# Gate scan: the final norm of both halves of the images done in turn at the end, instead of the first half's inside the last units of the scan

## What is computed

```
y = jnp.einsum('bdchw,d->bchw', out_y, w_m)
y = layernorm2d(y, ln_w, ln_b)      # (x - mean_c) / sqrt(var_c + 1e-5) * w + b, per pixel over 96 channels
y = grn(y, grn_gamma, grn_beta)     # Gx = sqrt(sum_hw x^2); Nx = Gx / (mean_c Gx + 1e-6)
                                    # gamma * x * Nx + beta + x
return conv1x1(y, W_out)            # 96 -> 48 channels
```

## Time and profile before

| | |
|---|---|
| time, median of 3 runs | 1013.42 us (1012.63 to 1014.58) |
| time of the profiled execution | 1012.31 us |
| span of the profiled execution | 1010.4 us |
| TensorE busy | 826.8 us (82%) |
| VectorE busy | 796.4 us (79%) |
| ScalarE busy | 573.6 us (57%) |
| GpSimd busy | 244.6 us (24%) |
| granted TensorE clock, mean | 0.866 of full speed |
| first products of unit 5, 6, 7 | 882.35, 912.97, 945.75 us |
| first final addition (L1021) | 969.47 us |

### The profile page before, as it was taken

The page is one execution under the profiler, slowest core; times in us unless marked ns, Lnnn a source line. Parts: engine busy times, 40 slices in busy tenths (PEclk is TensorE's granted clock), DMA queues, the critical chain, the costliest instruction groups (busy, mean ns, idle before and its releaser), DMA issues.

```text
span 1010.4 us, 20810 instructions
## 1 busy us (share of the span) xinstructions
PE 826.8 (82%) x8186; PEld 565.8 (56%) x8188; DVE 796.4 (79%) x2001; ACT 573.6 (57%) x859; POOL 244.6 (24%) x272
## 2 busy tenths in 40 slices
PE   3799999999999999999999988889577667353544
PEld 2577877887788778877777775365121111031222
DVE  8788888888888888888888874655539999888852
ACT  1376677676776776676666663123565664746002
POOL 6122222222222222222222221292201222115201
PEclk8799999999999999999999997979777755565656
DMA  8100000000000000002000000100003675566300
GB/s 234 49 2 2 2 2 2 2 1 2 2 2 2 2 2 2 2 1 102 1 3 2 2 2 1 47 1 1 1 1 63 126 133 114 100 123 125 77 2 16
DMA packets 11622, 34.14 MB, mean 34 GB/s; under 512 B 1879, under 2 KB 4359, under 8 KB 11271
## 3 DMA queue, kind: packets, MB, share of 16 engines
q0 software_dynamic: 5904, 21.24, 11.2%
q1 hardware_dynamic: 5623, 11.60, 3.9%
HBM read 10.81 MB, written 0.79 MB: 11 GB/s over the span
## 4 chain that ended last, share of the span: by engine, by line
PE 63%; DVE 22%; ACT 5%; issue 5%; POOL 2%; DMA 2%; POOLq 0%; SPq 0%; DVEq 0%; ACTq 0%
PE narrow L1453 5%; PE scores_a L1425 4%; PE wide L1376 4%; PE scores_b L1425 4%; PE last L1530 4%; PE scores_b L1412 3%; PE scores_a L1436 3%; PE scores_b L1436 3%; PE scores_a L1412 3%; PE narrow L1472 3%; PE narrow L1483 3%; DVE prod L991 3%; DVE prod L999 2%; PE last L1526 2%; PE wide L1516 2%
## 5 line engine op out<-in xcount | busy, mean ns | idle before, releaser
L376 POOL TENSOR_TENSOR stb<-stb,neg_half 128x4 f32<-128x4 f32 x48 | 48.3, 1006 | 266.1 <-DVE stb L679 266.1
L1104 ACT ACTIVATE d<-d 128x768 f32<-128x768 f32 x96 | 80.6, 839 | 18.1 <-DVE d L626 17.6
L1453 PEld LDWEIGHTS narrow<-v,pt 128*64 128x64 f32 x2304 | 78.7, 137 | 13.4 <-issue 13.4
L1453 PE MATMUL narrow<-v,pt 128*64 128x54 f32 x2304 | 84.9, 224 | 0.1
L371 POOL TENSOR_TENSOR sta<-sta,neg_half 128x4 f32<-128x4 f32 x48 | 48.8, 1017 | 115.7 <-DVE sta L566 115.7
L1111 ACT ACTIVATE pt<-scores_a 128x768 f32<-128x768 f32 x48 | 38.8, 809 | 56.7 <-PE scores_a L1436 56.7
L607 DVE COPY v<-narrow 64x96 f32<-64x96 f32 x192 | 49.0, 255 | 18.8 <-PE narrow L1388 13.8
L1120 ACT ACT_TABLE_LOAD x47 | 60.3, 1283 | 0.8
L1104 ACT ACT_TABLE_LOAD x46 | 59.0, 1283 | 0.8
L613 DVE TENSOR_REDUCE mx<-scores_a 128x12 f32<-128x768 f32 x48 | 46.0, 957 | 16.4 <-PE scores_a L1425 16.4
L1080 ACT ACTIVATE xa<-narrow,wts 113x256 f32<-113x256 f32 x48 | 27.0, 564 | 52.6 <-PE narrow L1363 27.8
(11 more groups left out here) (330 smaller groups left out, 2268.6 us busy)
## 6 DMA issues: line engine op xcount, KB each, us to landing
gsum<-mag POOLq DMA_DIRECT2D x14, 512.0 KB, 4.7
ysum<-yo POOLq DMA_DIRECT2D x7, 768.0 KB, 5.8
ysum<-xd POOLq DMA_DIRECT2D x6, 768.0 KB, 6.0
gsum<-mag POOLq DMA_DIRECT2D x14, 256.0 KB, 4.6
wts<-in_wpack SPq DMA_DIRECT2D x6, 442.0 KB, 6.9
sed_w<-in_sed_in SPq DMA_DIRECT2D x1, 2304.0 KB, 8.0
graw<-in_gates_in SPq DMA_DIRECT2D x1, 1152.0 KB, 5.0
x_all<-in_x_tok SPq DMA_DIRECT2D x8, 96.0 KB, 3.2
```

Source lines behind the costliest of these rows:

```text
L1104: act.activation(d, d, ACT.Exp).then_inc(p_ready[u], 1)
L1453: op = pe.matmul(y_ps[64 * b:64 * b + 64, q * VO:(q + 1) * VO], t.pt[:, q, h, 64 * b:64 * b + 64], t.v[:, q, b, h * VO:(h + 1) * VO], star ...
```

## The change

Half 0 is no longer normed inside units 5 to 7. All six TensorE stages, five VectorE stages and three ScalarE stages of both halves come after unit 7, stage by stage, half 0 then half 1. To let them be under way together, `tvar`, `rT` and `gx` exist twice, half 1's `yq` is a part of a gate tile (`gate[0][:, 0, :]`), half 1 uses banks 0 and 1 (scores_a) where half 0 uses 6 and 7, and each half has its own semaphores. TensorE's wait of half 1 for half 0's copies becomes one for ScalarE's having taken the last gate maps from banks 0 and 1. GpSimd issues the powers as both of `tail_rstd`, then both of `tail_norms`.

```diff
-        tvar = sb("tvar", [128, 2, 16])
-        rT = sb("rT", [16, 128])
-        gx = sb("gx", [128, 6, 8])
+        tvars = [sb(f"tvar{i}", [128, 2, 16]) for i in range(2)]
+        rTs = [sb(f"rT{i}", [16, 128]) for i in range(2)]
+        gxs = [sb(f"gx{i}", [128, 6, 8]) for i in range(2)]
+        yqs = [yq, gate[0][:, 0, :]]
+TAIL_BANK = (6, 0)
...
@@ GpSimd
-                if u == 5:
-                    tail_rstd(0)
-                if u == 6:
-                    tail_norms(0)
...
-            tail_rstd(1)
-            tail_norms(1)
+            for hb in range(2):
+                tail_rstd(hb)
+            for hb in range(2):
+                tail_norms(hb)
@@ VectorE, unit(u)
-                if u == 6:
-                    tail(0, (2,))
...
-                if u in (5, 6):
-                    tail(0, (0,) if u == 5 else (3,))
...
-                if u in (5, 6):
-                    tail(0, (1,) if u == 5 else (4,))
...
-            tail(1, range(5))
+            for stage in range(5):
+                tail(0, (stage,))
+                tail(1, (stage,))
@@ ScalarE
-                if u in (6, 7):
-                    tail(0, (u - 6,))
                 first_guess(u)
-            tail(0, (2,))
-            tail(1, (0, 1, 2))
+            for stage in range(3):
+                tail(0, (stage,))
+                tail(1, (stage,))
@@ TensorE
                     else:
-                        pe.wait_ge(out_ready, 2)
+                        for k in range(2):
+                            pe.wait_ge(gate_taken[k], (24, 21, 21)[k])
...
                 in_gates(u)
-                if u >= 5:
-                    tail(0, ((0,), (3,), (5,))[u - 5])
                 if u < 7 and u != 3:
                     gates(u + 1, (1, 2))
-                if u in (5, 6):
-                    tail(0, (1,) if u == 5 else (4,))
...
-                if u == 5:
-                    tail(0, (2,))
-            tail(1, range(6))
+            for stage in range(6):
+                tail(0, (stage,))
+                tail(1, (stage,))
```

More of the change, by code:

```diff
@@ L253, in build @@
         sum_ready = sems("sum_ready", 2)
-        tail_pe, tail_dve = sem("tail_pe"), sem("tail_dve")
-        yq_ready, trstd_ready, v_norm, gx2_ready, gx_ready, out_ready = (
-            sem(n) for n in ("yq_ready", "trstd_ready", "v_norm", "gx2_ready", "gx_ready", "out_ready"))
+        tail_pe, tail_dve = sems("tail_pe", 2), sems("tail_dve", 2)
+        tail_act, tail_pool = sems("tail_act", 2), sems("tail_pool", 2)
         block = ctx.enter_context(nc.Block())
@@ L1049, in tail @@
-                    step(dve.tensor_scalar(gx[:, 2, 0:2], B8[7][:, 0:2], 1.0 / DIN, 1e-6, ALU.mult, ALU.add))
-                    step(dve.reciprocal(gx[:, 3, 0:2], gx[:, 2, 0:2]))
-                    step(dve.tensor_tensor(per_group(4), per_group(1), gx[:, 3, 0:2].unsqueeze(1).to_broadcast([128, G, 2]), ALU.mult))
+                        return gxs[hb][:, k, 0:6].rearrange("p (g b) -> p g b", b=2)
+                    dve.wait_ge(tail_pe[hb], M_GM + 1)
+                    step(dve.tensor_scalar(gxs[hb][:, 2, 0:2], B8[TAIL_BANK[hb] + 1][:, 0:2], 1.0 / DIN, 1e-6, ALU.mult, ALU.add))
@@ L1052, in tail @@
+                    step(dve.reciprocal(gxs[hb][:, 3, 0:2], gxs[hb][:, 2, 0:2]))
+                    step(dve.tensor_tensor(per_group(4), per_group(1), gxs[hb][:, 3, 0:2].unsqueeze(1).to_broadcast([128, G, 2]), ALU.mult))
                     step(dve.tensor_tensor(per_group(2), per_group(4), l3w[:, Q_GRN:Q_GRN + G].unsqueeze(2).to_broadcast([128, G, 2]), ALU.mult))
-                    step(dve.tensor_scalar(gx[:, 5, 0:6], gx[:, 2, 0:6], 1.0, None, ALU.add))
+                    step(dve.tensor_scalar(gxs[hb][:, 5, 0:6], gxs[hb][:, 2, 0:6], 1.0, None, ALU.add))
@@ L1806, in tail @@
                             first = 512 * g + 128 * t
[L1807 removed]
+                            op = pe.matmul(B8[TAIL_BANK[hb]][:, 4 * t:4 * t + 4], yqs[hb][:, first:first + 128], l3w[:, Q_IND:Q_IND + 4],
                                            start=(g == 0), stop=(g == G - 1))
[L1809 removed]
+                    op.then_inc(tail_pe[hb], 1)
                 if 2 in stages:
[L1811 to L1812 removed]
+                    pe.wait_ge(tail_pool[hb], 1)
+                    pe.transpose(B8[TAIL_BANK[hb] + 1][0:16, 0:128], tvars[hb][:, 1, :], ident[:]).then_inc(tail_pe[hb], 1)
                 if 3 in stages:
[L1814 removed]
+                    pe.wait_ge(tail_dve[hb], D_RT + 1)
                     for t in range(4):
[L1816 to L1817 removed]
+                        op = pe.matmul(B8[TAIL_BANK[hb]][:, 128 * t:128 * (t + 1)], spread[:, t, :], rTs[hb][:], start=True, stop=True)
+                    op.then_inc(tail_pe[hb], 1)
                 if 4 in stages:
[L1819 removed]
+                    pe.wait_ge(tail_pool[hb], 2)
                     for g in range(G):
[L1821 to L1822 removed]
+                        op = pe.matmul(B8[TAIL_BANK[hb] + 1][:, 0:2], ones, gxs[hb][:, 1, 2 * g:2 * g + 2], start=(g == 0), stop=(g == G - 1))
+                    op.then_inc(tail_pe[hb], 1)
                 if 5 in stages:
```

77 lines of the change are left out of this document (33 added, 44 removed).

## The result

The changed kernel takes 1005.1 us (median of 6 runs, 1003.27 to 1008.76) against 1013.3 us for the kernel before in the same session: ratio 0.9923, 95% interval 0.9898 to 0.9948. A second session gave 1004.5 us against 1013.55 us, ratio 0.9904 (0.9869 to 0.9938). The forecast was 1006.0 us, which is a ratio of 0.9927 to the 1013.42 us it was made against. The profiled execution took 1003.27 us with a span of 1001.4 us; the forecast for a profiled execution was 1004.8 us.

A forecast was written before the change was run, and what follows sets the result against it. VectorE's own instructions were taken to bound the scan's units, a relay between engines the tail. Removing 15.74 us and adding 8.2 us gave -7.5 us: median 1006.0 us from 1013.42, range 1002.5 to 1011.0 us.

The forecast's parts named there:

- The 15.74 us: Units 5 and 6: their excess over a 23.83 us unit without the norm, all forecast to go.
- the five detours: VectorE's waits and work for half 0's norm in units 5 and 6, read as 15.8 us together.
- The cover of 2.3 us: In unit 1 ScalarE's Exps end 2.3 us before VectorE needs them; some 2 us expected in units 5 and 6.
- The rival of the magnitude DMAs: Units 5 and 6: late DMAs stall VectorE's first reciprocal step, from 2.3 us extra delay; up to 1021.6 us; chance 0.03.
- The tail, +8.2 us: From the first final addition to the end: 49.1 us instead of 40.93, so 8.2 us more.
- the squares, which the text says add 0.7 us net: TensorE's 24 passes per half after the column sums: end forecast at 14.4 us, 0.7 us net added.
- four passes of the output were low: Tail output: first four passes at the low clock, 0.85 us each, the rest 0.43; both halves 12.2 us.
- "In one line" of the prediction: Summary of the tail's extra 8.2 us: squares +0.7, copy -0.4, ScalarE +4.65, missing scaling -2.0, second output +5.2.
- GpSimd held up (0.11): Tail rival: VectorE's scaling of half 0 delays half 1's power of the norms, +1.7 us, 1007.7 us; chance 0.11.
- The text's own sign of being wrong: The 128x6 GpSimd power in the tail lasting longer than 1.4 us would show the forecast wrong.
- Low clock through the output (0.06): Tail rival: all 24 output passes at the low clock, 20.5 us instead of 12.2, 1014.2 us; chance 0.06.
- Little overlap (0.04): Tail rival: half 1 waits through every half 0 stage, tail grows 29.2 us instead of 8.2, 1026.9 us; chance 0.04.

The follow-up runs named there:

- e5_late45: e4_bufs with only half 0's last two stages (sums of the norms with scaling, output) and GpSimd's root moved behind the scan: 1008.81 us, ratio 0.9953.
- e2_nohalf0: Changed kernel with half 0's norm stages taken out of every engine's stream, its output stored unnormed: 997.72 us, ratio 0.983.
- e3_serial: Changed kernel with all of half 0's stages ahead of all of half 1's in each stream, no alternation: 1027.75 us, ratio 1.0131.
- e1_again: The changed kernel run once more, nothing changed: ratio 0.9904 to the kernel before, tail 47.75 us.
- e4_bufs: Changed kernel's second set of tiles, banks and semaphores, but the order of the kernel before: 1013.27 us, ratio 0.999.
- e12_port3: e4_bufs with two GpSimd fills of 128x384 between unit 6's last magnitude DMA and half 0's root: 1012.27 us, ratio 0.9979.
- e7_split2: As e6_split, but half 0's multiplication by the spread also inside unit 7 and its scaling behind half 1's subtraction: 999.72 us, ratio 0.9851.
- e6_split: Changed kernel reordered: half 0's column sums to transpose inside units 5 to 7, VectorE's a unit late, the rest in the tail's gaps: 999.54 us, ratio 0.9859.
- e8_warm: Changed kernel with extra unread bf16 matmuls in TensorE's gaps, before the last addition, after the spreads and after half 0's sums: 1004.47 us, ratio 0.9902.

## Why the prediction was right

- **The 15.74 us.** Exact: units 5 and 6 came down by 15.74 us, and e5_late45 confirms one of the five detours alone (6.15 for 6.2 us); e2_nohalf0 and e3_serial have the same unit times. The argument that a unit without the norm is VectorE's own 23.7 us of work carried it.
- **The cover of 2.3 us.** It was 3.3 and 3.6 us, more than in unit 1. The rival of the magnitude DMAs did not come near its point.
- **The tail, +8.2 us.** It was +7.24 us. The term that was mis-sized is the first one: column sums and squares together ended at 13.6 us instead of 14.4. The clock rose within the column sums (they took 4.83 us, not 5.46), and the high level gave 0.114 us a pass in the squares, not 0.13. So the squares, which the text says add 0.7 us net, added nothing: half 1's end at 13.6 us, and at 13.7 us in the kernel before. The rest of the list is off by 0.1 us at most. That four passes of the output were low, as taken, is partly luck: when the clock rises differs from run to run. In e1_again the same tail took 47.75 us, so the term is too high by some 1.0 to 1.4 us.
- **"In one line" of the prediction** (squares +0.7, copy -0.4, ScalarE +4.65, scaling -2.0, output +5.2). These terms are counted against the kernel before, and there they come to +7.24 us. Against the same kernel without half 0 the sum is 6.1 us, since without half 0's output the clock rises later in half 1's (8.45 us). The kernel before's own tail is steady: 40.93 us, and 40.99 and 40.64 us in e4_bufs and e12_port3, which have its order.
- **GpSimd held up (0.11)** did not happen; 1.44 us against 1.32. The text's own sign of being wrong, a power longer than 1.4 us, came up all the same: it was set too tight, since the scaling cost the power 0.12 us without holding it until it ended. **Low clock through the output (0.06)** did not happen either: four low passes and twenty high ones, as taken. **Little overlap (0.04)** is what the kernel does when the alternation is taken away, at 29.3 us for the 29.2 of the text, a match that is partly luck (e3_serial).
- **The median.** 1005.1 for 1006.0 us, an error of the size of the tail's. The kernel before came out at 1013.3 against 1013.42 us. Executions scatter by some 6 us, so that the medians agree to less than 1 us is partly luck; the stretches above are the better evidence.

## What to carry to other kernels

A piece of a later stage put into an engine's stream costs that engine its work and also the wait for its input; cut the trace at the repeating unit and compare a unit with and without the piece, and the cost stands there (6.15 us measured for 6.2 read). Two independent relays over many engines should be alternated stage by stage (7 us for the second relay here, 29 us in turn), and better still, the stages of the one that is ready early go into the other's units one unit late, where they cost work alone (115.1 and 114.5 instead of 119.5 us). A matmul stage that fills a gap ahead of the critical one can give time back through the clock, but not reliably: it did in e7_split2, on the output it did not in e6_split, and the extra matmuls of e8_warm brought nothing.

## What the runs showed of the hardware

- A GpSimd power of 128x6 that takes 1.32 us alone took 9.64, 9.64 and 8.35 us beside VectorE's scan steps (kernel before, e4_bufs, e12_port3), each time until 1.21 us after those steps ended, and an addition of 128x6 took 10.70 us, until 0.06 us after them. Four powers like it took 1.45 to 1.81 us beside the start of the same steps, and the steps kept their pace.
- The squares' passes (a 128x128 weight load and four columns) take 0.114 us at 2.4 GHz and 0.219 us at 1.2 GHz. The clock can fall in the middle of them while TensorE has no gap: in e1_again it was busy from 954.98 us on, with the column sums and then these passes, and the granted clock was 1.00 from 961.5 to 961.9 us and 0.50 from 961.92 us on. In e8_warm it stood at 1.2 GHz up to 995 us, though TensorE had worked since 979.6 us with gaps under 1 us.
